# Fused graph layer on one core: seven more edge groups on the table of normalised rows, its gathers paced, scatters issued in pairs

## What is computed

```python
h = jnp.maximum(_layernorm(x, axis=-1), 0.0)
em = jnp.concatenate([h[src], h[dst]], axis=-1)
em = relu(layer_norm(em @ msg_w + msg_b, msg_g, msg_beta)) * edge_weights[:, None]
msgs = segment_sum(em, dst, N)                   # and counts: edges per node
messages = msgs / (counts + 1e-08) * (counts > 0)
gate = sigmoid(h @ gate_w + gate_b)
combined = jnp.concatenate([h, messages], axis=-1)
h_new = relu(layer_norm(combined @ upd_w + upd_b, upd_g, upd_beta))
out = x + gate * h_new + (1.0 - gate) * h
```

## Time and profile before

| | |
|---|---|
| median of 3 timed runs | 991.21 us (989.0 to 993.62) |
| the profiled execution, its own time | 981.87 us |
| its span, first to last instruction | 980.1 us |
| DVE busy / ACT busy | 873.4 us (89%) / 852.0 us (87%) |
| PE busy / POOL busy | 698.9 us (71%) / 673.0 us (69%) |
| mean granted clock of PE | 0.706 |
| indirect transfers issued by POOL | 392 gathers, 196 scatters, 3 of the tail |

### The profile page before, as it was taken

How to read it: one execution, slowest core, us unless ns; L and a number is a source line. 1 busy time by engine, 2 the same in 40 slices (tenths; PEclk the granted TensorE clock), 3 DMA queues, 4 the chain that set the end, 5 groups by cost and what they waited for, 6 DMA issues and landing times.

```text
span 980.1 us, 19229 instructions
## 1 busy us (share of the span) xinstructions
PE 698.9 (71%) x3696; PEld 547.5 (56%) x3696; DVE 873.4 (89%) x3834; ACT 852.0 (87%) x3678; POOL 673.0 (69%) x602
## 2 busy tenths in 40 slices
PE   2377787877777777886766377777867878687781
PEld 1255555555555555554555266666756766576661
DVE  7299999999989999999995379999998888879984
ACT  3299999999989999999996389999989888779963
POOL 4667777776876877878747566766766666666557
PEclk9655655565555555556567698999899889889976
DMA  5246666666666667667523112333221111111111
GB/s 150 90 147 216 203 215 218 204 222 204 227 223 213 215 219 239 222 220 237 174 67 103 51 43 88 97 98 97 77 75 65 64 59 62 65 64 60 57 70 34
DMA packets 74260, 133.65 MB, mean 136 GB/s; under 512 B 15846, under 2 KB 17718, under 8 KB 74194
## 3 DMA queue, kind: packets, MB, share of 16 engines
q1 hardware_dynamic: 53868, 97.58, 28.6%
q0 software_dynamic: 18912, 34.84, 13.0%
q10 hardware_dynamic: 1414, 0.53, 0.2%
HBM read 56.01 MB, written 80.81 MB: 140 GB/s over the span
## 4 chain that ended last, share of the span: by engine, by line
ACT 45%; DVE 23%; issue 12%; PE 9%; another core or an unknown queue 6%; POOL 3%; ACTq 1%; DVEq 0%; DMA 0%; POOLq 0%; SPq 0%
ACT junk L410 13%; ACT hrow L403 9%; ACT work L437 8%; DVE work L458 5%; DVE work L469 5%; ACT xload L403 4%; POOL out L615 3%; DVE work L480 3%; ACT lnv L385 3%; DVE st L357 3%; ACT work L1134 2%; DVE work L475 2%; ACT rs L390 2%; PE pm L1273 2%
## 5 line engine op out<-in xcount | busy, mean ns | idle before, releaser
L615 POOL DMA_INDIRECT out<-work,sidx x196 | 201.4, 1027 | 128.0 <-issue 55.0
L1221 PE MATMUL pt<-ident,hrow 128*128 128x128 f32 x508 | 128.3, 401 | 128.9 <-ACT hrow L403 108.8
L610 POOL DMA_INDIRECT ring<-in_x,gidx x140 | 171.0, 1221 | 60.7 <-issue 41.1
L437 ACT ACTIVATE work<-work,gt 128x128 f32<-128x128 f32 x588 | 200.7, 413 | 3.7 <-DVE work L475 3.3
L1255 PE MATMUL py<-w_u,work 128*128 128x129 f32 x784 | 200.0, 434 | 0.0
L1255 PEld LDWEIGHTS py<-w_u,work 128*128 128x128 f32 x784 | 171.6, 322 | 39.2 <-issue 39.2
L610 POOL DMA_INDIRECT ring<-in_x,src_i x116 | 143.0, 1233 | 46.4 <-issue 34.4
L1221 PEld LDWEIGHTS pt<-ident,hrow 128*128 128x128 f32 x508 | 84.8, 202 | 159.3 <-ACT hrow L403 135.6
L410 ACT ACTIVATE junk<-py 128x128 bf16<-128x128 f32 x588 | 152.5, 278 | 18.5 <-remote 14.0
L469 DVE SCALAR_TENSOR_TENSOR work<-py,rs,g_upd 128x128 f32<-128x128 f32 x588 | 162.9, 336 | 4.2 <-ACT rs L390 4.2
L403 ACT ACTIVATE hrow<-xload,nb,rs 128x128 f32<-128x128 f32 x392 | 161.9, 489 | 3.0 <-DVE nb L396 2.7
(11 more groups left out here) (172 smaller groups left out, 1631.9 us busy)
## 6 DMA issues: line engine op xcount, KB each, us to landing
xload<-in_x SPq DMA_DIRECT2D x98, 256.0 KB
normalised_rows<-hrow SPq DMA_DIRECT2D x98, 256.0 KB
out<-work SPq DMA_DIRECT2D x98, 256.0 KB
running_sums<-acc SPq DMA_DIRECT2D x49, 256.0 KB
staged_target_rows<-work SPq DMA_DIRECT2D x14, 256.0 KB
ring<-staged_target_rows SPq DMA_DIRECT2D x14, 256.0 KB
out<-work,sidx POOLq DMA_INDIRECT x196
ring<-in_x,gidx POOLq DMA_INDIRECT x140
```

The source lines that it names most:

```text
L437: last = nc.scalar.activation(t_buf[:, g.at % 4, k, :], t_buf[:, g.at % 4, k, :], ACT.Relu, scale=gt[:, g.at % 4, k:k + 1])
L610: pool.indirect_dma_start(out=dest, out_offset=None, in_=rows, in_offset=bass.IndirectOffsetOnAxis(ap=idx, axis=0), **({} if rows is sums_ ...
L615: pool.indirect_dma_start(out=out, out_offset=bass.IndirectOffsetOnAxis(ap=idx, axis=0), in_=rows, in_offset=None, **if_tail).then_inc(s, 16)
L1221: last = nc.tensor.transpose(dest[:, k * H:(k + 1) * H], rows[:, k, :], ident[:, :])
```

## The change

The constants move: `LATE` from 29 to 22, `UPFRONT` from 10 to 13. So groups 22 to 28 take their source rows from the `h` table too. Their 28 gathers leave the node phase. Behind the table's completion now stand 52 gathers (groups 22 to 34), in turns of six, three behind the first half of `flip` of group `turn` and three behind the second. In the iterations, the third scatter waits for `msg` of group g+6, and the refills wait for the first half of `flip` of group g+7.

```diff
-LATE = 29
-UPFRONT = 10
+LATE = 22
+UPFRONT = 13
@@
-            for g in range(LATE, LATE + UPFRONT):
-                if g >= RING:
+            upfront = [(g, k) for g in range(LATE, LATE + UPFRONT) for k in range(G)]
+            for i, (g, k) in enumerate(upfront):
+                turn, part = divmod(i, 6)
+                if part == 0:
+                    ed["flip"].after(pool, Group(turn), 1)
+                elif part == 3:
+                    ed["flip"].after(pool, Group(turn))
+                if g >= RING and k == 0:
                     ed["h"].after(pool, Group(g - RING), 1)
-                for k in range(G):
-                    gather_src(g, k)
+                gather_src(g, k)
@@
                 ed["flip"].after(pool, Group(min(g + 6, EG - 1)))
                 for k in range(G):
+                    if k == 2 and g + 6 < EG:
+                        ed["msg"].after(pool, Group(g + 6))
                     c = g * G + k
                     scatter(o[:, g % 4, k, :], sidx[:, c:c + 1], s_scat[g % 4])
+                if g + 7 < EG:
+                    ed["flip"].after(pool, Group(g + 7), 1)
```

## The result

| | before | after |
|---|---|---|
| median (4 runs each) | 990.11 us (986.09 to 993.62) | 1013.17 us (1010.99 to 1016.8) |
| ratio, 95% interval | | 1.0237 (1.0192 to 1.0281) |
| the profiled execution, its span | 981.87, 980.1 us | 1014.84, 1013.2 us |
| DVE / ACT / PE / POOL busy | 873.4 / 852.0 / 698.9 / 673.0 us | 870.0 / 845.0 / 716.2 / 668.7 us |
| mean granted clock of PE | 0.706 | 0.685 |

The change is slower by 23 us, 2.4%, well over the 0.5% that a measurement can tell. The forecast was 1006, slower. The two spans lie 33.1 apart, because the execution profiled before was a quick one (8 us under the median of 990.11) and the one after was not.

A forecast was written before the change was run, and what follows sets the result against it. POOL's unbroken issue, holding back PE's signals, was taken as the bound: 508.2 + 71.2 + 4 + 291.8 + 32.4 + 89.8 = 997.4 against 980.1, put on the median 991.2 + 15 = 1006 us; range 966 to 1021.

The forecast's parts named there:

- POOL's ledger: POOL's transfers and pauses from 508.20 us on; 12 gathers and 16 refills more there, together 39.1 us.
- the last 13 iterations: End of the kernel, without refills: left at 89.8 us, with up to 12 of 17 us of pauses able to go.
- The run of gathers: First table gathers, from 508.2: 52 x 1.37 (71.2) plus three pauses (4 us), first scatter near 583.
- This stall goes off PE and DVE without POOL being earlier: Run of gathers: turns of six remove a stall of 5.4 + 17.1 us, entered as no gain for POOL.
- Line 1134 has no step above 16 us between 520 and 585: Sign at ACT's copy in the run of gathers: the step of 25.72 us should shrink to 14 or so.
- signals come out when POOL stops: Edge phase: PE's signals are late while POOL issues without pause; ACT goes on about 1.1 us after POOL stops.
- The pauses of the iterations: POOL's 36 iterations, three waits each: pauses of 0.9 us per iteration, 32.4 us, where 1.43 stood.
- Rival A: Waits in POOL's run let PE's signals through, pauses 0.3 per iteration: 973 us, faster; chance 0.35.
- Rival B: The waits free nothing, each of POOL's iterations pauses 1.43 as before: 1024 us; chance 0.16.
- C: More work and fewer pauses on POOL cancel, pauses about 0.4 to 0.6 per iteration: 986 to 996 us; chance 0.13.
- D: Stall in the run of gathers is slow landings or instruction loading; sum changes under 5 us; no chance of its own.
- PE mostly has its 2.4 GHz level: PE's granted clock, 0.91 behind the run of gathers and 0.70 in it, with dips to 1.2 GHz following idle times.

The follow-up runs named there:

- The run with the signals through: The unaltered change measured again, in a session where PE's signals reach other engines without delay: 935.19 us against 910.11, ratio 1.028.
- the staging kernel: Before with LATE 32, UPFRONT 7 and two more groups of target rows staged in the node phase (STAGED 16): 912.73 us, ratio 1.0023.
- LATE 22 without turns: The change without its turns of six, pairs and third wait kept: 1023.7 us, ratio 1.0355 to before.
- LATE 22 alone: Before with only LATE 22 and UPFRONT 13, none of the new waits: 1030.77 us, ratio 1.0405; in a later session 933.35 us, ratio 1.0253.
- the first four experiments: LATE 22 and UPFRONT 13 without waits, the waits at LATE 29, LATE 32 with UPFRONT 7, the change without turns: 1030.77, 986.43, 972.73, 1023.7 us.
- LATE 32: Before with LATE 32 and UPFRONT 7, 12 gathers moved into the node phase, no new wait: 972.73 us, ratio 0.9819.

## Why the prediction was right, and where it wasn't

**The direction and the main term held.** POOL's ledger was the right account: 39 us of transfers more, in the place where POOL is the bound, less what pauses give back. The run with the signals through is the cleanest test of it, since no pause blurs the sum there; as no trace of before is kept from such a session, its terms are estimates. 12 gathers x 1.40 = 16.8 longer run, 16 refills x 1.40 = 22.4 longer iterations, and the last 13 iterations 15 us shorter, because POOL comes to them late and finds every wait met (73.4 us, where the staging kernel takes 88.9 for them at DVE's pace). 16.8 + 22.4 - 15.5 = 23.7, and 25.1 was measured. The amount in the comparison itself, 23 against the 15 I had put on the median, owes something to chance: there the last 13 iterations gave back nothing (91.9 for 89.8), the iterations gave back 12 us of pauses, and the turns took the place of a wait that I had not seen.

**The run of gathers** was forecast at 75.2 and took 76.5; three pauses of 4.4 for the 4 I had entered. First scatter 588.42 for 583, of which 3.7 lies ahead of 508.20. That term isn't the change's: among the six traces with held signals the first table gather stands at 507.65 to 512.82, and with the same node phase at 507.65 (LATE 22 without turns), 511.93 and 512.82. It is the scatter of single executions.

**"This stall goes off PE and DVE without POOL being earlier" is the sentence that failed.** It took the stall for free time. Without the turns DVE falls so far behind that POOL waits 13.4 to 14.1 us for it when the gathers are out. The turns reduce that to 4.4, and the comparison of the ratios puts them at 12 us. The sum came out near all the same, because I compared with before, which has 6.9 of the same kind; by my terms a kernel without turns should have been up to 4 us faster than the change, and it was 12 slower.

**"Line 1134 has no step above 16 us between 520 and 585"** was wrong: 20.4 us at 524.48, and 25.9 at 586.54, just behind the stretch. I expected pacing to let the signals out, but a turn of six bites only when DVE is behind, and behind the gathers POOL had scatters for which every wait was already met. And the reading under it, that signals come out when POOL stops, holds for the late steps (1.0 and 1.1 us after the last transfer) and not for the run of gathers. I called the copy of 534.80 "the same", yet in the trace of before POOL issues without a break from 508.20 to 557.58, and that signal came out in the midst of it:

```profile
534.40 1.00 POOL L610 DMA_INDIRECT ring<-normalised_rows,src_i  x1 [0.30 <-issue]
```

**The pauses of the iterations** are the mis-sized term. I took 0.9 each, 32.4; they were 39.4, 1.09 each, and that is 7 of the 15.8 us by which the profiled span exceeds the sum. (Between the medians only 8 us are missing, 23 for 15: the other 8 are the quick execution profiled before.) The rest: 3.7 ahead of the gathers, 1.3 in them, 1.7 for longer transfers (293.5 for 291.8), 2.1 at the end. Also the cause was put wrongly: of the fall from 1.43 to 1.09, the longer iterations alone bring 0.19 (1.24 in LATE 22 alone) and the waits at most the other 0.15.

**Rival A** (the signals get through, 973 us) did not come about in the comparison. Its condition, a pause below 0.47 per iteration, was met in full in the second run of the change, with 0; and there the change is no faster but 2.8% slower. The rival's error was mine: it gave the changed kernel the freed signals and left before with the held ones. **Rival B** (pauses stay 1.43, 1024 us) is out by the 1.09, but not by much: iteration 36 starts at 921.3, between my 908 and its 931, and 1013 lies 7 above my figure and 11 below its. **C** did not occur; of **D** nothing is shown, and that instruction loading holds the signals isn't excluded.

The prediction also said that PE mostly has its 2.4 GHz level. That was misread: up to 495 us the granted clock is 0.56, behind 566 us 0.89, and 0.706 in the mean. No term of the sum used it.

**What holds PE's signals is open.** I read it as the effect of POOL's unbroken issue. In the held traces every long stall begins in such a row, the longest (30.8 us of ACT's wait, in LATE 22 alone) ends 1.9 us after the 52nd gather, and at 20 to 47 us, where POOL issues 20 gathers in one row, three waits of ACT for PE are marked `remote`:

```profile
29.85 0.28 ACT L410 ACTIVATE junk<-py 128x128 bf16<-128x128 f32 x1 [4.50 <-remote]
...
34.82 0.60 ACT L1083 ACTIVATE work<-pt 128x512 f32<-128x512 f32 x1 [3.37 <-remote]
...
46.80 0.28 ACT L410 ACTIVATE junk<-py 128x128 bf16<-128x128 f32 x1 [9.40 <-remote]
```

But several stalls end while POOL issues on (534.80 before, 544.88 and 612.41 after, 545.82 in LATE 22 alone), so the end of the row is not what lets the signals out. And the same kernels issue the same rows in other sessions without any holding. So a row of transfers is at most one of several conditions, and no run here shows the others. The expectation of the second change run speaks of another chip. The record doesn't bear that out: it gives the chip the same number, 9, in the session of the first four experiments (before at 988) and in that of the second change run (before at 910), and 5 and 2 in the other two. The Trainium skill (SBUF — State Buffer, section Who interferes with whom) has PE waiting for no one. The traces with the signals through agree, 0.13 us from the end of a turn to its reader; those with held signals don't, up to 18.4 us in the trace of the change. The page speaks of ports, and what is late here is the signal, not the matmul.

## What to carry to other kernels

Count the instructions of the engine that issues the transfers from the point where it becomes the bound, and ask of an edit first how many it puts behind that point: 28 transfers moved there cost 23 to 25 us where signals come through, with the waits or without them, and 23 to 43 where they are held, by the waits that were added. An engine whose idle column is nothing but its issue gap is the bound even at 73% busy. And a time lost by an engine off the path isn't free if the bound engine will later wait for it: the 13 to 14 us of the first scatter came from a stall that looked harmless. When a rival frees a resource in the changed kernel, free it in the kernel before as well before comparing.

## What was not expected of the hardware

- The same program takes 988 or 911 us by session. For the change the difference (1013.2 and 932.6 us of span) lies at every stage: 24.8 us up to the first table gather, 3.7 in the run of gathers, 33.6 in the iterations, 18.5 behind.
- Where signals are held, PE's come in their order, one by one, also while POOL issues: after the turn of 531.10 ACT's copy reads it at 544.88, and the turn of the sums, finished 0.4 us later, is read 2.1 us after that. Where they come through, that of the turn of the sums is recorded 0.01 to 0.02 us after the matmul's end.
- Which kernel is best depends on it: LATE 32 is 1.8% faster than before with held signals; where they come through, its three variants (with the waits, with the staging, with earlier refills) are 0.2 to 0.4% slower, and the plain one wasn't run. Moving work off POOL pays only while POOL is the bound, and by these runs before stands about at the balance when the signals come through.
- A 128-row transfer costs POOL 1.0 us and 0.30 of issue at its best, but its mean was 1.06 to 1.11 in the iterations of the kernels, with no order that the edits explain; over 200 transfers that alone is 10 us.
